# A gated cross-attention block: feed-forward rows padded to six blocks of 128, and two VectorE steps moved

## The reference

```
q = layernorm(x) @ Wq.T + bq;  k = ctx @ Wk.T + bk;  v = ctx @ Wv.T + bv
s = clip(q k / 4, -50, 50), masked entries set to -50;  p = softmax(s) per head
delta = layernorm(rs * (p v @ Wo.T + bo)) * gamma + beta
x1 = x + tanh(g_xattn) * delta
n = aq(layernorm(x1))
h = silu(n @ wq(w1).T) * (n @ wq(w2).T)            # 100 x 704
out = x1 + tanh(g_ffn) * (aq(h) @ wq(w3).T)
aq(a) = round(a * s) / s, s = 127 / max|a| of the row;   wq(w) = three levels, -1, 0, 1, times mean|w|
```

## Time and profile before

| | us |
|---|---|
| median of 3 runs | 1439.22 (1439.09 to 1439.60) |
| the profiled execution, its own time | 1438.62 |
| its span in the trace | 1436.8 |
| TensorE matmuls busy | 1348.5 (94%), 19984 instructions |
| TensorE weight loads busy | 1220.3 (85%), beside the matmuls |
| VectorE busy | 1131.2 (79%) |
| ScalarE busy | 965.1 (67%) |
| GpSimd busy | 469.7 (33%) |
| TensorE's granted clock, mean | 0.974 of full |

### The profile page before, as it was taken

How to read it: one execution, slowest core, us unless ns; L and a number is a source line. 1 busy time by engine, 2 the same in 40 slices (tenths; PEclk the granted TensorE clock), 3 DMA queues, 4 the chain that set the end, 5 groups by cost and what they waited for, 6 DMA issues and landing times.

```text
span 1436.8 us, 48034 instructions
## 1 busy us (share of the span) xinstructions
PE 1348.5 (94%) x19984; PEld 1220.3 (85%) x19984; DVE 1131.2 (79%) x2241; ACT 965.1 (67%) x1634; POOL 469.7 (33%) x759
## 2 busy tenths in 40 slices
PE   5699999999999999999999999999999999999982
PEld 5599888888988888898888898888889888888971
DVE  6668788878878887877887887888788788878763
ACT  2367776676776767777676777767777767676751
POOL 3523333233333223233323333332333332232310
PEclk9699999999999999999999999999999999999995
DMA  7467666666766666776667676666667666766620
GB/s 217 110 160 174 157 153 156 164 158 167 169 163 155 154 163 166 168 169 156 156 152 171 161 176 160 158 150 161 163 162 173 158 157 155 167 163 162 139 52 8
DMA packets 142477, 222.13 MB, mean 155 GB/s; under 512 B 29162, under 2 KB 135598, under 8 KB 142254
## 3 DMA queue, kind: packets, MB, share of 16 engines
q1 hardware_dynamic: 129966, 199.31, 57.7%
q0 software_dynamic: 12288, 19.69, 6.2%
HBM read 54.00 MB, written 3.28 MB: 40 GB/s over the span
## 4 chain that ended last, share of the span: by engine, by line
PE 52%; DVE 25%; ACT 13%; issue 7%; POOL 2%; SPq 1%; DMA 0%; DVEq 0%; POOLq 0%; ACTq 0%
PE pvb L1212 13%; PE sc L1192 12%; PE cb L1233 11%; PE cb L1247 9%; ACT e_sb L549 7%; DVE e_sb L783 4%; DVE zt L855 3%; DVE c_lo L750 2%; PE mb L1280 2%; PE mb L1271 2%; DVE tiny L935 2%; PE mb L1298 2%; DVE k_lo L774 2%; DVE th L945 1%; ACT us L623 1%
## 5 line engine op out<-in xcount | busy, mean ns | idle before, releaser
L549 ACT ACTIVATE e_sb<-sc 121x800 f32<-121x800 f32 (+1 forms) x768 | 644.8, 844 | 201.4 <-PE sc L1192 191.3
L1192 PE MATMUL sc<-q_st,k_st 96*121 96x200 f32 (+1 forms) x3072 | 476.4, 278 | 7.1 <-DMA q_st<-bd_hi 3.1
L1192 PEld LDWEIGHTS sc<-q_st,k_st 96*121 96x121 f32 (+1 forms) x3072 | 416.3, 186 | 42.5 <-issue 9.0
L783 DVE TENSOR_SCALAR e_sb<-e_sb,hi_b 121x1600 f32<-121x1600 f32 (+1 forms) x384 | 399.4, 1047 | 38.3 <-ACT e_sb L549 38.1
L1212 PE MATMUL pvb<-e_sb,v_sb 121*32 121x100 f32 x12288 | 286.2, 251 | 0.1
L1212 PEld LDWEIGHTS pvb<-e_sb,v_sb 121*32 121x32 f32 x12288 | 264.7, 110 | 22.6 <-issue 19.0
L774 DVE SCALAR_TENSOR_TENSOR k_lo<-cb,bk_c,k_hi 128x484 fp32r<-128x484 f32 (+1 forms) x192 | 134.4, 700 | 137.8 <-ACT k_hi L561 137.8
L1247 PE MATMUL cb<-wv_hi,c_hi 128*121 128x256 f32 (+1 forms) x768 | 227.8, 297 | 15.2 <-DVE k_lo L774 12.2
L475 POOL DMA_DIRECT2D q_st<-bd_hi x256 | 183.2, 719 | 107.9 <-DVE bd_lo L829 104.7
L1247 PE MATMUL cb<-wv_hi,c_lo 128*121 128x256 f32 (+1 forms) x768 | 217.0, 283 | 0.0
L1247 PE MATMUL cb<-wv_lo,c_hi 128*121 128x256 f32 (+1 forms) x768 | 216.9, 282 | 0.0
(11 more groups left out here) (139 smaller groups left out, 1609.0 us busy)
## 6 DMA issues: line engine op xcount, KB each, us to landing
k_st<-k_hi SPq DMA_DIRECT2D x512, 121.0 KB, 2.8
c_in<-in_ctxT SPq DMA_DIRECT2D x64, 484.0 KB, 3.8
k_st<-k_lo SPq DMA_DIRECT2D x256, 121.0 KB, 2.9
k_st<-k_hi SPq DMA_DIRECT2D x256, 119.0 KB, 2.3
c_in<-in_ctxT SPq DMA_DIRECT2D x32, 476.0 KB, 3.6
k_st<-k_lo SPq DMA_DIRECT2D x128, 119.0 KB, 2.4
q_st<-bd_hi POOLq DMA_DIRECT2D x256, 50.0 KB, 3.3
q_st<-bd_lo POOLq DMA_DIRECT2D x128, 50.0 KB, 3.2
```

The costliest lines, as they stand in the source:

```text
L549: nc.scalar.activation(e_sb[e_slot(b, n)][0:TL[n], k * SW:(k + 1) * SW].rearrange("p (o c) -> p o c", o=2), sc[q % NSC][0:TL[n], :, 0:2 * PW],
L783: V.tensor_scalar(e, e, E_LO, hi_b[b.par][0:TL[n], n:n + 1], ALU.max, ALU.min).then_inc(clip_done, 1)
L1192: last = T_.matmul(sc[q % NSC][0:TL[n], e // 2, (e % 2) * PW:(e % 2 + 1) * PW], k_st[st_slot(b, n // TPC)][:, pr // NQ, pr % NQ, t0:t0 + T ...
```

## The change

The hidden row hq is widened to 768 = 6 x 128 columns, the last 64 set to zero once at the start. So all six transposes are of 128 columns, all six matmuls of `down` over 128 rows (the last block of w3 is filled with zeros already), and ScalarE copies hT in one instruction. On VectorE, `result(b - 2)` goes ahead of clip 1 in step 2, and `split_rest` of chunk 0 moves from step 1, behind clip 0, to step 2, behind clip 1. The other two chunks stay in steps 5 and 9.

```diff
--- before.py
+++ after.py
@@ -173,7 +173,7 @@
         x2T = sb("x2T", [P, KT, S], bf16)
         th_p, gs_p, us_p = sb("th", [P, F]), sb("gs", [P, F]), sb("us", [P, F])
         th, gs, us = th_p[0:S, :], gs_p[0:S, :], us_p[0:S, :]
-        hq = sb("hq", [S, F], bf16)
+        hq = sb("hq", [S, FT * P], bf16)
         hT = sb("hT", [P, FT, S], bf16)
         y_out = sb("y_out", [S, H])
 
@@ -228,7 +228,7 @@
                     "ha0", "hb0", "ha1", "hb1", "hmax", "hinv", "hs", "hround", "hq", "cy")
         D_P = Steps("var", "rstd", "r", "var2", "rstd2", "ct", "cu")
         D_T = Steps("delta", "x2T", "g0", "u0", "g1", "u1", "hT", "y")
-        D_A = Steps("x2T", "t0", "g0", "u0", "t1", "g1", "u1", "hTa", "hTb")
+        D_A = Steps("x2T", "t0", "g0", "u0", "t1", "g1", "u1", "hT")
 
         pieces = [slice(a, min(a + H, CW)) for a in range(0, CW, H)]
         GUARD_C = Steps(*(f"{u}{k}{i}{c}" for u in range(NCH) for k in range(KT) for i in range(len(pieces))
@@ -398,6 +398,7 @@
         def _(pool):
 
             nc.gpsimd.memset(e_sb[2][:, (FT - 1) * H:FT * H], 0.0)
+            nc.gpsimd.memset(hq[:, F:FT * P], 0.0)
             nc.gpsimd.memset(e_sb[3][0:TT, (NT - 1) * NB:NT * NB], 0.0).then_inc(s_setp, 1)
             nc.gpsimd.memset(identf[:, :], 0.0)
             nc.gpsimd.memset(identb[:, :], 0.0)
@@ -606,9 +607,8 @@
 
             def h_turned(b):
                 act.wait_ge(pe_post, D_T.after(b, "hT"))
-                v = mb16[:, 0:FT * S].rearrange("p (k s) -> p k s", k=FT)
-                nc.scalar.activation(hT[:, 0:FT - 1, :], v[:, 0:FT - 1, :], ACT.Copy).then_inc(act_post, 1)
-                nc.scalar.activation(hT[0:FL, FT - 1, :], v[0:FL, FT - 1, :], ACT.Copy).then_inc(act_post, 1)
+                nc.scalar.activation(hT[:, :, :], mb16[:, 0:FT * S].rearrange("p (k s) -> p k s", k=FT), ACT.Copy
+                                     ).then_inc(act_post, 1)
 
             def ffn_gate(b, i):
                 act.wait_ge(pe_post, D_T.after(b, f"g{i}"))
@@ -946,7 +946,7 @@
 
             def h_quant(b):
                 d_wait(b, "hround")
-                dv(V.tensor_scalar(hq[:, :], th[:, :], MAGIC, QMAX, ALU.subtract, ALU.min))
+                dv(V.tensor_scalar(hq[:, 0:F], th[:, :], MAGIC, QMAX, ALU.subtract, ALU.min))
                 dv(V.tensor_scalar(tiny[:, 10:11], tiny[:, 8:9], k_y[0:S, :], None, ALU.mult))
 
             def result(b):
@@ -988,13 +988,15 @@
                             attention_out(d)
                         if n == 10:
                             hidden_gate(d, 0)
+                    if prev2 and n == 2:
+                        result(b.plus(-2))
                     if n:
                         clip(b, n - 1)
                     elif prev:
                         clip(d, NT - 1)
                     if nxt and n == 6:
                         q_rest(c)
-                    if nxt and n % 4 == 1:
+                    if nxt and n in (2, 5, 9):
                         split_rest(c, n // 4)
                     if b.base:
                         w = n - (ITEM + 1) + (0 if n > ITEM else NT)
@@ -1004,8 +1006,6 @@
                         hidden_up(b.plus(-2), 1)
                         for step in (h_max, h_scale, h_round, h_quant):
                             step(b.plus(-2))
-                    if prev2 and n == 2:
-                        result(b.plus(-2))
                     if nxt and n == 2:
                         x_stats(c)
                     if nxt and n == 3:
@@ -1302,15 +1302,13 @@
             def h_turn(b):
                 pe.wait_ge(dve_post, D_V.after(b, "hq"))
                 for k in range(FT):
-                    m = P if k < FT - 1 else FL
-                    last = T_.transpose(mb16[0:m, k * S:(k + 1) * S], hq[:, k * P:k * P + m], identb[0:S, 0:S])
+                    last = T_.transpose(mb16[:, k * S:(k + 1) * S], hq[:, k * P:(k + 1) * P], identb[0:S, 0:S])
                 last.then_inc(pe_post, 1)
 
             def down(b):
-                pe.wait_ge(act_post, D_A.after(b, "hTb"))
+                pe.wait_ge(act_post, D_A.after(b, "hT"))
                 for k in range(FT):
-                    m = P if k < FT - 1 else FL
-                    last = T_.matmul(mb[0:S, 0:H], hT[0:m, k, :], w3q[0:m, k, :], start=k == 0, stop=k == FT - 1)
+                    last = T_.matmul(mb[0:S, 0:H], hT[:, k, :], w3q[:, k, :], start=k == 0, stop=k == FT - 1)
                 last.then_inc(pe_post, 1)
 
             def batch(b, own, nxt, prev, prev2):
```

## The result

| | before | after |
|---|---|---|
| median of 4 runs, us | 1439.41 (1439.09 to 1439.96) | 1459.59 (1456.77 to 1461.06) |
| ratio to before, with 95% interval | | 1.0137 (1.0119 to 1.0156) |
| profiled execution, us (its span) | 1438.62 (1436.8) | 1458.22 (1456.4) |
| granted clock of TensorE, mean | 0.974 | 0.958 |

A forecast was written before the change was run, and what follows sets the result against it. VectorE's chain to `dl`, not TensorE, was taken to set each lap: 29 x 0 + 1.07 - 0.18 - 0.56 = +0.33 us on 1438.62, so 1438.95, or 1439.5 as the runs' median; range 1434 to 1442.5 us.

The forecast's parts named there:

- The lap: Each batch runs from `x_turn` to the last exponential, then VectorE's work to `dl`: 26.2 and 16.0 us.
- What is late next is thus `dl`, and it takes all of it.: At `x_turn`, TensorE's shortened waits gather into one of some 1.5 us for `dl`; no gain per batch.
- The padding's 0.18 us: Full blocks remove the gap before the sixth weight load of `down`: 0.18 us of TensorE per batch, covered by `dl`.
- The second batch: There `attention_read` already waits for TensorE, so moving c_lo behind that wait adds 1.07 us ahead of `dl`, once.
- The tail: `down` is on the path at the end: 0.18 us less in the last batch, 0.56 over the last two feed-forwards.
- c_lo as cover: Slower rival: `attention_read`, moved earlier, waits for unfinished matmuls in every batch; 1470 us, likely 1454; chance 0.06.
- nothing replaces the wait: Rival: the gap at `x_turn` is TensorE's own, so 29 batches give back 0.75 and 0.18 us; 1412 us; chance 0.07.
- only the padding pays: Rival: TensorE's own time sets part of the lap; removing 0.18 us in 29 batches gives 1434 us; chance 0.07.
- The transfers: On SyncE's queue, the third chunk's load, the store and the key stack behind c_lo's later end: cost 0.
- What I had named as the sign of being wrong: A shorter lap with a small wait at L1264, or `attention_read` waiting for TensorE in every batch.
- L844 <- PE pvb: A wait of VectorE for TensorE's pv bank which, if seen in every batch, would show the slower rival.

The follow-up runs named there:

- e4_sum_only: Kernel before with only the final sum moved ahead of clip 1, no padding and c_lo left in step 1: 1439.00 us, ratio 1.0001.
- e8: Changed kernel with the row statistics right behind the final sum in step 2, and xn and dl ahead of clip 2 in step 3: 1426.45 us, ratio 0.9916.
- e9: e8 with k_lo of chunk 0's second half also moved on VectorE, from step 6 to ahead of x1_norm in step 5: 1404.87 us, ratio 0.9768.
- e1_fill: Changed kernel with 24 small unused matmuls on TensorE just before the transpose of x, where it waits for dl: 1440.58 us, ratio 1.0011.
- e2_split: Changed kernel with one more TensorE wait, delta in step 3 waiting for clip 1, so the idle time comes in two pieces: 1438.94 us, ratio 1.0005.
- e3_moves: Kernel before with both VectorE moves (final sum ahead of clip 1, c_lo behind it) but without the padding: 1440.79 us, ratio 1.0011.
- e7_clo_only: Kernel before with only c_lo (the remainder of chunk 0) moved to step 2, behind clip 1: 1440.14 us, ratio 1.0010.
- e6: Kernel before with both VectorE moves, no padding, and only the first three of six blocks in `down`; a test only: 1459.36 us, ratio 1.0139.
- e5: Kernel before with the padding alone (768 columns, six full blocks, one copy of hT), VectorE's order as before: 1442.84 us, ratio 1.0034.

## Why the prediction was wrong

- **The lap.** Right, and shown: `x_turn` was late because of `dl`, the sum's move gave nothing (e4_sum_only), laps without a fall are 42.20 us, and shortening VectorE's chain shortens them (e8, e9).
- **"What is late next is thus `dl`, and it takes all of it."** This is the step that failed. I added up the waits that would gather at `x_turn`, some 1.5 us, and priced them at zero, because their sum did not change. What they do to the granted clock was nowhere in the sum. A wait of mostly 1.8 us cost 1.3 us in 12 of 29 laps and 2.9 in one, where the clock stayed down twice as long. Without the fall (e1_fill) the same order takes 1440.6 us, with the waits apart (e2_split) 1438.9; my 1439.5 was the price of the order alone. The page of the Trainium skill on this, "TensorE: Matmul & The Clock Gate", HAM oscillation, describes loops that lose the fast clock in every pass by waiting for transfers. The trace agrees that waits inside a loop can cost the fast clock, and differs in two points: waits of 1.8 us, shorter than the page warns of, are enough, and only 13 of 29 passes lose it. There the measurement decides.
- **The padding's 0.18 us.** Mis-sized: 0.59 us. It alone decides between e3_moves (1.2 us at `x_turn`, no fall) and the changed kernel (1.8 us, 13 falls). With the right size I would have had 1.9 us instead of 1.5.
- **The second batch.** +1.07 forecast, +1.41 measured; +1.17 in e7_clo_only, and from +0.6 (e1_fill) to +2.1 (e3_moves) in e1, e2, e3 and e6, which have c_lo moved too. One profiled execution each, so the sign is shown and the size only roughly.
- **The tail.** -0.74 forecast (0.18 and 0.56). From the last `x_turn` to the end of the span it takes 105.5 us against 105.4 before, and between 104.4 and 107.0 in e1 to e5 and e7, padded or not. The term doesn't show above this scatter.
- **c_lo as cover.** `attention_read` waits in no steady batch of the changed kernel; that rival is refuted, and so are "nothing replaces the wait" and "only the padding pays".
- **The transfers.** Priced at nothing, rightly: the context load goes out at 789.11, the store at 789.53 and the stack of keys at 790.03 in the batch shown, and neither e1_fill nor e7_clo_only loses anything to them.
- **What I had named as the sign of being wrong** (a shorter lap, or "L844 <- PE pvb") did not include a longer lap at an unchanged wait pattern. None of my rivals was the clock.

Still open: why the clock falls in about half of the laps and not in all, at equal waits of 1.8 us. The fall comes at different distances behind the wait, from the very start of `x_turn` to 1.8 us behind it (the query's eight matmuls are slow wholly, partly or not at all), so it seems to hang on where the wait lies in time. No run here was made to settle it.

## What to carry over

When TensorE's waits are not the bound, moving them is not free: add up how much idle time comes to lie together before you gather several short waits into one, and look at the granted clock microsecond by microsecond behind the longest. A change that makes TensorE arrive earlier at a wait it can't shorten can cost more than it could ever have saved; shorten what it waits for first (here VectorE's chain to `dl`), which is where the time was: 34 us less than the kernel before in e9_klo_early. Read what a removed odd-sized tile is worth from load to load across its neighbours, not from the gap that the view names.

## What the hardware showed that I had not expected

- The granted clock of TensorE fell to half after a single wait of 1.6 to 2.1 us (mostly 1.8) between stretches of full work, in 13 of 29 laps (16 of 29 in e6_short_down), and after two waits of 0.67 and 0.77 us with 1.0 us of work between them in 5 of 29. No lap showed a fall with one wait of mostly 1.1 to 1.2 us (e3_moves, e7_clo_only, 29 laps each), nor with 0.56 and 0.96 us and 3.3 us of work between (e2_split, 29 laps).
- A fall costs 1.6 us on the stretch behind it (4.95 instead of 3.35 us in most of the long laps), and 1.3 us of a lap; 0.3 us of it is taken up further on.
- A 64-row matmul and a 64-column transpose among full ones cost 0.33 and 0.26 us of TensorE beyond their full-sized counterparts.
- GpSimd's 1/sqrt on 100 numbers took 0.57 us alone and 1.34 us beside VectorE's subtraction of two SBUF tiles.
